# The last, 53-row block of the value products: contracted over 128 rows padded with zeros, or over its own 53 rows

## The reference

```
q, k, v = (x @ Wq + bq), (x @ Wk + bk), (x @ Wv + bv)    # per head, C = 128
alpha = einsum(q[dst], k[src]) / sqrt(C)                  # one score for each edge
p = exp(alpha - segment_max(alpha)[dst])
out = segment_sum(p * v[src], dst) / (segment_sum(p, dst) + 1e-16)
return out + x @ Ws + bs
h = relu(conv(x, layer 1, 4 heads, concatenated))
result = layernorm(x + conv(h, layer 2, 2 heads, mean))
```

## Time and profile before

| | us |
|---|---|
| median of 3 runs | 2024.7 |
| lowest and highest | 2024.05, 2025.37 |
| the profiled execution | 2025.37 |
| its span in the trace | 2023.2 |
| PE busy | 1827.1 (90%) |
| PE weight loads busy | 1526.9 (75%) |
| DVE busy | 1594.0 (79%) |
| ACT busy | 1241.2 (61%) |
| POOL busy | 1161.6 (57%) |

### The profile page before, as it was taken

One profiled execution on the slowest core, in us unless ns is written; L12 is line 12 of the kernel. 1 busy time (PEld: TensorE's weight loads), 2 busy tenths in 40 slices (PEclk: granted clock), 3 DMA queues, 4 the chain that ended last, 5 costly groups with the idle time before them and its releaser, 6 DMA issues. The chain is left out here.

```text
span 2023.2 us, 44524 instructions
## 1 busy us (share of the span) xinstructions
PE 1827.1 (90%) x14788; PEld 1526.9 (75%) x14788; DVE 1594.0 (79%) x4609; ACT 1241.2 (61%) x2055; POOL 1161.6 (57%) x1481
## 2 busy tenths in 40 slices
PE   2866667999999999999999999949789999999998
PEld 1456556888888888888888888836578888888887
DVE  3899987888888888888888888723488888888886
ACT  2655445777777777777767776711156666756666
POOL 3410004776777677677777676611257777777775
PEclk7877778999999999999999999969889999999999
DMA  5059985787787778778887877680169899899995
GB/s 122 0 140 229 228 222 120 154 155 146 156 152 150 149 153 154 149 149 153 156 152 143 158 155 149 110 227 3 51 127 176 166 182 174 173 171 180 170 178 110
DMA packets 771457, 303.29 MB, mean 150 GB/s; under 512 B 657154, under 2 KB 751086, under 8 KB 767979
## 3 DMA queue, kind: packets, MB, share of 16 engines
q1 hardware_dynamic: 767323, 296.42, 72.5%
q10 hardware_dynamic: 3266, 2.36, 0.5%
q0 software_dynamic: 640, 1.63, 0.3%
HBM read 94.57 MB, written 48.45 MB: 71 GB/s over the span
## 5 line engine op out<-in xcount | busy, mean ns | idle before, releaser
L1330 PE MATMUL score_l<-KT,QT_l 128*125 128x512 f16 (+2 forms) x3150 | 774.8, 356 | 15.5 <-DVE piece_max_l L1185 15.2
L1185 DVE CUSTOM_DVE_ANT_0 prob_l<-score_l,mask_l 125x512 f32<-125x512 f32 (+2 forms) x1050 | 642.5, 614 | 179.5 <-PE score_l L1330 178.0
L1034 POOL TENSOR_TENSOR prob_parts_l<-prob_l,prob_parts_l 125x512 f16<-125x512 f32 x600 | 722.4, 1234 | 16.8 <-ACT prob_parts_l L1113 16.8
L1104 ACT ACTIVATE prob_l<-prob_l,neg_max_l 125x1024 f32<-125x1024 f32 (+1 forms) x450 | 524.3, 1165 | 119.6 <-DVE neg_max_l L1193 119.5
L1361 PE MATMUL output_l<-V,prob_flipped_l 128*125 128x256 f16 x2400 | 465.8, 275 | 1.3 <-DMA prob_flipped_l<-prob_parts_l 1.3
L1330 PEld LDWEIGHTS score_l<-KT,QT_l 128*125 128x125 f16 x3150 | 370.4, 139 | 95.3 <-DVE piece_max_l L1185 19.1
L1363 PE MATMUL output_l<-V,prob_flipped_l 128*125 128x128 f16 x2400 | 433.2, 219 | 0.0
L1119 ACT CAST probT_l<-transposed_l 128x375 f16<-128x375 f32 x450 | 209.9, 466 | 347.8 <-PE transposed_l L1355 347.8
L1022 POOL CAST QT_l<-q_now_l 128x125 f16<-128x125 f32 x150 | 53.8, 358 | 545.0 <-ACT q_now_l L1091 545.0
L1363 PEld LDWEIGHTS output_l<-V,prob_flipped_l 128*125 128x125 f16 x2400 | 333.1, 139 | 15.7
L1361 PEld LDWEIGHTS output_l<-V,prob_flipped_l 128*125 128x125 f16 x2400 | 328.6, 137 | 18.2 <-issue 2.1
(11 more groups left out here) (166 smaller groups left out, 2001.7 us busy)
## 6 DMA issues: line engine op xcount, KB each, us to landing
mask_scratch<-log SPq DMA_DIRECT2D x79, 448.0 KB
mask_l<-mask_scratch SPq DMA_DIRECT2D x50, 448.0 KB
mask_l<-mask_scratch SPq DMA_DIRECT2D x24, 896.0 KB
mask_l<-mask_scratch SPq DMA_DIRECT2D x24, 471.2 KB
prob_flipped_l<-prob_parts_l SPq DMA_TRANSPOSE x600, 3.2
mask_l<-mask_scratch SPq DMA_DIRECT2D x24, 336.0 KB
hT_scratch<-rowsT_l SPq DMA_DIRECT2D x25, 250.0 KB, 3.6
hT<-hT_scratch SPq DMA_DIRECT2D x6, 1024.0 KB, 13.6
```

The costliest lines, as they stand in the source:

```text
L1034: pool.tensor_tensor(parts[0:TP, 1, a:b], prob[:, h % 2, a:b], parts[0:TP, 0, a:b], ALU.subtract).then_inc(s_flo, 1)
L1104: act.activation(e, e, ACT.Exp, bias=neg_max[:, h % 2:h % 2 + 1], accum_out=total[:, h % 2, c:c + 1]).then_inc(s_exp, 1)
L1185: dve.tensor_tensor_reduce(out=prob[:, h % 2, a:b], in0=score_bank(h, p)[0:TP, 0:b - a], in1=mask[:, parity, a:b], scale=1.0, scalar=-3.0e ...
L1330: last = pe.matmul(score_bank(h, p)[0:TP, 0:b - a], QT[:, h % 2, i, :], KT[:, h, j, a:b], start=n == 0, stop=n == len(products) - 1)
```

## The change

`product` reads V, and `values` reads `probT`, on the first `width_of(b)` partitions alone. For blocks 0 to 23 that is 128 as before. For block 24 it is 53, in both operands of both matmuls. The two clears of V's last block are taken out, since the rows that they cleared are no longer read.

```diff
@@ mask_and_projections, vector
                 dve.tensor_scalar(few[:, :], bank[CHUNK_BANK][0:1, WG:WG + 1], float(E), None, ALU.is_equal).then_inc(s_few, 1)
-                link(dve.memset(V[:, NT - 1, :, :, :], 0.0))
@@ attention, tensor
                 def product(h, b, hi, lo, start=False, stop=False):
-                    pe.matmul(O[0:TP, 0:2 * C], hi, V[:, b, h, :, :].rearrange("p a c -> p (a c)"),
+                    w = width_of(b)
+                    pe.matmul(O[0:TP, 0:2 * C], hi, V[0:w, b, h, :, :].rearrange("p a c -> p (a c)"),
                               start=start, stop=False, skip_group_check=True)
-                    return pe.matmul(O[0:TP, 0:C], lo, V[:, b, h, 0, :], start=False, stop=stop, skip_group_check=True)
+                    return pe.matmul(O[0:TP, 0:C], lo, V[0:w, b, h, 0, :], start=False, stop=stop, skip_group_check=True)
@@ values
-                        hi, lo = (probT[:, q, n, i * TP:(i + 1) * TP] for n in range(2))
+                        hi, lo = (probT[0:width_of(b), q, n, i * TP:(i + 1) * TP] for n in range(2))
```

## The result

The changed kernel takes 2048.77 us, median of 4 runs (2047.49 to 2052.8), against 2025.03 for the kernel before (4 runs, 2024.05 to 2029.19). The ratio is 1.0116 with a 95% interval of 1.0097 to 1.0137: 23.7 us slower, where 42 were forecast. The profiled execution took 2046.03.

What follows compares the result with a forecast made beforehand. PE was taken as the bound, so nothing on it is hidden: 2025.4 us profiled + 42 (0.28 us in each of 150 steps) - 0 for the clears = 2067.4, forecast 2067 us, 2.1% slower; range 2038 to 2083.

Steps and rivals of the forecast that it cites:

- The forecast proper: Whole run: both changes of array part in each step cost 0.12 to 0.18 us, giving 2060 to 2080 us; chance 0.65.
- What the clears give: The two DVE clears of V's last block: taken as 0; if both were exposed, 0.75 us or 0.04%.
- Fewer rows shorten nothing: Block 24's 300 matmuls with 53 rows: same columns, so no time saved; 75 rows took 165 ns, 128 rows 164.
- A change of the part lets the array run empty, both ways: On PE, into and out of block 24's 64 x 128 part: a hole each way, 0.28 us a step, 42 us.
- The first rival: No price at block 24: the array's rows are switched without a hole, as for transposes; 2024 to 2025 us; chance 0.12.
- the second: Only going out of block 24's narrow part costs, 21 us, so 2046; chance 0.14 for one way or partly hidden.
- The price of 0.138 us a change: At block 24, streaming begins 0.194 us after the start of the matmul before instead of 0.056: loss 0.138, say 0.14.
- I take nothing as hidden: PE's wait for probT in slot 4: a later PE starts that chain later, so all 42 us are seen.
- As the busy time of PE shows: PE's 47 us of weight-load waits for probT: mostly hidden behind a streaming matmul, read from busy 983.8 of 996.7 us.
- The bound of 12.9 + 5.7 us of idle time: PE's idle time in the two layers' attention could be used up: 42 - 19 = 23 us left, about 2048.
- Two further signs: Over the run: PE's busy share falls a little, and DVE's wait for scores grows by about 40 us.
- The third and fourth rivals: Block 24: half time with fewer rows, 2012 us, chance 0.03; full-end waits or lower clock, 2089 and above, chance 0.06.

Runs made afterwards that it cites:

- the edit on ACT alone: Kernel before, full rows, with ACT's copy of the turned rows moved ahead of its third exponential in head 0 of layer 1: 2019.39 us, ratio 0.9958.

## Why the prediction was right in its range and too high

- *The range*: it held, but not for the reason given. The forecast proper, both prices seen in full at 2060 to 2080, missed. The lower end of 2038 had been put there to take in a price paid one way only, and that is not what happened.
- *PE is the bound and DVE has nothing to give*: right. What the clears give is below what the runs can tell.
- *Fewer rows shorten nothing*: right, with 96 rows at a ratio of 1.0005.
- *A change of the part lets the array run empty, both ways*: right in all 150 steps. The first rival (no price) and the second (one way only) are refuted by the timeline, though the second's 2046 us is near the measured 2048.8. The number alone would have led to the wrong cause. That starts inside block 24 would keep 0.11 was wrong for the first matmul, which has 0.160: it is the 0.05 for the first weights, which the price already counts.
- *The price of 0.138 us a change*: right, 0.142 and 0.139 measured.
- *"I take nothing as hidden"*: this is the step that failed. It looked at one wait alone, that for probT, and at the chain of its own step from slot 2 to slot 4. What hid the price stood elsewhere: lateness of DVE that is carried over from head 2's last slot into head 3 (and from head 1 into head 0 in layer 2), held by POOL and not by PE, and a wait of the skip product two slots behind the holes. The waits that went are 0.27 us in 25 steps twice, and 0.15 in 25 more: 17 us of 42, which leaves 25 against 23.7 measured. The prediction had said that a layer 1 growing by much less than 28 us, with the holes there, would prove it wrong on the chain. Layer 1 grew by 12.9.
- *"As the busy time of PE shows"*: the reading behind that step, and busy time can't show it. PE's records run to modelled ends, so they cover a part of each wait. Layer 1 from the first skip product to the last (length; busy us of PE, PEld, DVE, ACT, POOL; clock, DMA, GB/s), in the kernel before, with the edit on ACT alone, and in the changed kernel:

```profile
334.53:1296.54 962.01, 954.67 (x8019) 806.72 (x8018) 791.78 (x2617) 683.89 (x1176) 679.38 (x889) 1.00 0.78 150
337.50:1292.90 955.40, 950.38 (x8020) 806.25 (x8018) 791.82 (x2617) 683.87 (x1176) 679.52 (x888) 1.00 0.80 151
334.85:1309.68 974.83, 971.88 (x8019) 810.37 (x8018) 779.64 (x2617) 683.85 (x1176) 673.76 (x889) 1.00 0.77 148
```

  Taking the skip product's wait away made the stretch 6.6 us shorter and PE's idle time only 2.3 us less (7.3 to 5.0). In the changed kernel 14 us of the price were hidden here and the idle time fell by 4.4 (to 2.9).
- *The bound of 12.9 + 5.7 us of idle time* gave 2048, which is the result, by luck. In layer 2 the idle time went from 5.7 to 4.6 us over its 24 tiles, so only 5.4 us of idle time were used up in both layers, where some 17 us of price were hidden.
- *Two further signs*: PE's busy share rose from 90 to 91% in place of falling, since a hole of this size lies under the modelled ends. DVE's wait for scores did grow by about 40 us as foretold, from 178.0 to 223.3 over the run, but not for the reason given: the span grew by half of that, and the rest is DVE's busy time, which fell from 1594.0 to 1571.3 us, since its clears, less held up by POOL, took 263.8 us in place of 287.6.
- *The third and fourth rivals*, a gain and a price above 0.2: neither came. The starts inside block 24 came no closer. The granted clock of the run was 0.949, before 0.947.

## What to carry to other kernels

A cost put on the engine that bounds the kernel is seen in full only where no wait of that engine comes behind it that something else holds; count those waits by step, over the whole period of the loop, and take them off before forecasting. Read them from the distances between starts: the skip product's load came 0.28 us (median) behind the start of the last matmul before it, and beside it once the wait was gone. PE's idle time showed only a third of that wait. And a contraction cut to its true rows is not a saving on TensorE: zeros up to a row count that keeps the neighbours' part of the array (96 rows here) cost nothing that could be measured, and 64 or 53 rows cost 0.14 us at each change.

## What was new about the hardware

- Two plain matmuls that name different parts of the array lose 0.139 to 0.142 us between them at the granted clock of 2.4 GHz, measured for rows (64 x 128 against 128 x 128) behind a matmul of 128 columns: the load starts 0.07 to 0.08 us before the modelled end of the matmul before. For columns (128 x 64) the loads have 0.16 and 0.17 us of idle time. Transpose instructions with 53 weight columns have none.
- A DVE mask clear of 309 columns (both inputs in SBUF) took 0.99 to 1.27 us, ending 0.33 to 0.34 us behind the POOL subtraction that ran beside it: its length tells when it was issued and not what it costs, which is 0.48 us with nothing of POOL beside it.
- A wait that the profile puts down to "issue" can be a wait on a semaphore all the same: the 0.3 us ahead of the skip product went when ACT's copy was moved.
